# Third attention of a fused network: output stores on GpSimd's queue, relative products moved within a head, transposes of the probabilities three steps behind

## What is computed

```python
def _L2_attn_ref(x, Wq, Wk, Wv, Wo, pek, pev):   # HD = 8, MAX_LEN = 128, SCALE = HD ** 0.5
    Q, K, V = (proj(Wq), proj(Wk), proj(Wv))
    scores = jnp.einsum('bhqd,bhkd->bhqk', Q, K) / SCALE
    idx = _rel_idx(s)                            # clip(k - q, -128, 128) + 128
    rel_k = pek[idx]
    scores = scores + jnp.einsum('bhqd,qkd->bhqk', Q, rel_k) / SCALE
    scores = jnp.where(causal[None, None], scores, -jnp.inf)
    attn = jax.nn.softmax(scores, axis=-1)
    out = jnp.einsum('bhqk,bhkd->bhqd', attn, V)
    rel_v = pev[idx]
    out = out + jnp.einsum('bhqk,qkd->bhqd', attn, rel_v)
    return out.transpose(0, 2, 1, 3).reshape(b, s, D) @ Wo.T
```

## Time and profile before

| | us |
|---|---|
| Median of 3 runs | 4655.31 (4641.95 to 4663.07) |
| The profiled execution, its own time | 4653.93 |
| Its span | 4652.1 |
| The stage `relative_heads`, about | 2555 to 3527 of the span |

### The profile page before, as it was taken

One profiled execution on the slowest core, in us unless ns is written; L12 is line 12 of the kernel. 1 busy time (PEld: TensorE's weight loads), 2 busy tenths in 40 slices (PEclk: granted clock), 3 DMA queues, 4 the chain that ended last, 5 costly groups with the idle time before them and its releaser, 6 DMA issues. The chain is left out here.

```text
span 4652.1 us, 70787 instructions
## 1 busy us (share of the span) xinstructions
PE 3257.9 (70%) x22883; PEld 1799.3 (39%) x22883; DVE 2404.9 (52%) x4948; ACT 1877.1 (40%) x4450; POOL 684.5 (15%) x964
## 2 busy tenths in 40 slices
PE   5588544374435777778775777777783288849998
PEld 3344233253322444444443333333332122227776
DVE  4565466455655666666642445445455488821111
ACT  2355322211113455554542444444441177723332
POOL 2100000120003444444422000000000300000000
PEclk8798766686667899999986666666665599969999
DMA  4323000000001000000004777777772522220000
GB/s 118 64 48 62 23 0 0 8 1 5 0 9 47 17 17 9 17 17 17 17 9 138 188 190 192 190 192 191 193 195 72 137 42 53 40 69 1 0 0 18
DMA packets 423549, 303.19 MB, mean 65 GB/s; under 512 B 60175, under 2 KB 396234, under 8 KB 423250
## 3 DMA queue, kind: packets, MB, share of 16 engines
q1 hardware_dynamic: 414034, 278.32, 24.3%
q0 software_dynamic: 6912, 18.88, 1.3%
q10 hardware_dynamic: 2304, 2.36, 0.2%
HBM read 148.98 MB, written 133.18 MB: 61 GB/s over the span
## 5 line engine op out<-in xcount | busy, mean ns | idle before, releaser
L1139 DVE TENSOR_REDUCE a_soft_NM<-a_soft_s_ps 128x2 f32<-128x1024 f32 (+3 forms) x512 | 514.5, 1021 | 204.2 <-PE a_soft_s_ps L1074 132.3
L1173 ACT ACTIVATE a_soft_PTS<-a_soft_st_ps 128x512 f32<-128x512 f32 (+3 forms) x1024 | 458.3, 522 | 148.1 <-PE a_soft_st_ps L1050 100.9
L464 PE MATMUL a_soft_pt_ps<-net_ident,a_soft_PR 128*128 128x128 f32 x1280 | 328.7, 369 | 110.0 <-ACT a_soft_PTS L566 103.5
L612 ACT ACTIVATE a_soft_PR<-a_soft_s_ps,a_soft_least 128x128 f32<-128x128 f32 (+3 forms) x512 | 263.7, 526 | 342.3 <-DVE a_soft_least L587 237.9
L1045 PE MATMUL a_soft_st_ps<-a_soft_QS,a_soft_KS 50*128 50x512 bf16 (+4 forms) x1024 | 258.7, 360 | 59.4 <-ACT a_soft_PTS L1173 33.3
L1954 ACT ACTIVATE f_run_HT<-f_run_h_ps 128x512 f32<-128x512 f32 x256 | 152.8, 597 | 290.7 <-PE f_run_h_ps L1921 290.7
L1968 DVE SCALAR_TENSOR_TENSOR net_X<-f_run_y_ps,f_COEF,net_X 128x128 f32 x256 | 72.1, 344 | 381.2 <-PE f_run_y_ps L1930 381.2
L464 PEld LDWEIGHTS a_soft_pt_ps<-net_ident,a_soft_PR 128*128 128x128 f32 x1280 | 182.6, 180 | 208.7 <-ACT a_soft_PR L612 146.2
L1930 PEld LDWEIGHTS f_run_y_ps<-f_W,f_run_HT 128*128 128x128 f32 x2048 | 237.5, 192 | 26.8 <-issue 26.8
L1087 PE MATMUL a_soft_o_ps<-a_soft_PTS,a_soft_VR 128*32 128x512 f32 (+3 forms) x2048 | 242.6, 548 | 0.1
L2104 PE MATMUL f_run_ps<-f_run_WQKV,f_run_HT 128*128 128x512 f32 x384 | 229.6, 689 | 15.5 <-DVE f_run_RS L1402 8.3
(11 more groups left out here) (356 smaller groups left out, 6517.4 us busy)
## 6 DMA issues: line engine op xcount, KB each, us to landing
a_soft_BIAS<-skew_d SPq DMA_DIRECT2D x256, 191.0 KB, 4.2
band_d<-a_soft_PR SPq DMA_DIRECT2D x256, 191.0 KB, 3.7
skew_d<-a_soft_RS SPq DMA_DIRECT2D x128, 256.0 KB, 4.4
a_soft_PB<-band_d SPq DMA_DIRECT2D x128, 256.0 KB, 3.1
a_soft_QS<-query_rows_d SPq DMA_DIRECT2D x32, 384.0 KB, 9.6
query_rows_d<-a_proj_PARTS SPq DMA_DIRECT2D x72, 128.0 KB, 3.5
query_rows_d<-a_proj_PARTS POOLq DMA_DIRECT2D x72, 128.0 KB, 3.0
key_rows_d<-a_proj_PARTS SPq DMA_DIRECT2D x72, 128.0 KB, 3.9
```

The lines of the kernel that those rows point to most:

```text
L464: last = pe.transpose(pt_ps[:, slot, kb * P:(kb + 1) * P], PR[:, n % NPR, OFF + kb * P:OFF + (kb + 1) * P], ident[:])
L612: act.activation(PR[:, n % NPR, OFF:OFF + width(j)], s_ps[:, n % 4, 0:width(j)], ACT.Exp, bias=least[:, n:n + 1], scale=-1.0).then_inc(pro ...
L1139: dve.tensor_reduce(NM[:, T % 2, j, p, :], s_ps[:, ring["s", a] % 2, :, 0:width(j)], AX.X, ALU.max, negate=True).then_inc(max_ready, 1)
L1173: act.activation(PTS[:, T % 2, 2 * p + par, kb, q0:S], st_ps[:, e % 3, q0:S], ACT.Exp, scale=scale).then_inc(probs_ready, 1)
```

## The change

Four things move. The stores of the outputs are issued by GpSimd (POOL) instead of ACT, one quad at a time, after ACT has copied them. PE makes the relative products in step 3 of a head instead of step 0, and ACT copies them after the exponential of step 3 instead of before that of step 1. SP stores them after the stores of the band instead of before the load of a bias. And PE turns the probabilities three steps behind instead of two (`LAG`); which of a head's five turns falls to DVE and which to ACT stays as it was by position, so each engine gets other widths. No work is added or dropped.

```diff
@@ sync: quad
-                    for f, a in ((store_rel, 3), (load_bias, 2)):
-                        if not (final and h + a >= 4):
-                            f(hd + a, (h + a) % 4, qd if h + a < 4 else qd + 1)
+                    if not (final and h >= 2):
+                        load_bias(hd + 2, (h + 2) % 4, qd if h < 2 else qd + 1)
                     store_band(hd, h, qd)
+                    if not (final and h >= 1):
+                        store_rel(hd + 3, (h + 3) % 4, qd if h < 1 else qd + 1)
@@ gpsimd
-            batches(quad, lambda: None, pool)
+                if prev:
+                    store(qd - 1, 1 - u % 2, *((b, u - 1) if u else (b - 1, 3)))
+
+            def store(qd, sl, b, u):
+                pool.wait_ge(o_copied, qd + 1)
+                for h in range(4):
+                    pool.dma_start(out_d[ds(b, 1), 4 * u + h].rearrange("a r f -> (a r) f"),
+                                   OS[32 * h:32 * h + HD + 1, sl, :]).then_inc(o_stored[sl], 16)
@@ tensor: quad
-                    if j == 0 and not (final and h >= 1):
+                    if j == 3 and not (final and h >= 1):
                         uu, hh = (u, h + 3) if h < 1 else ((u + 1) % 4, h - 1)
                         relative(b if h < 1 or u < 3 else b + 1, uu, hh, 4 * qd + h + 3)
...
-                    if n >= 2:
-                        turn(qd, n - 2, h, pos, qd)
+                    if n >= LAG:
+                        turn(qd, n - LAG, h, pos, qd)
                     elif prev:
-                        turn(qd - 1, n + 14, h, pos, qd)
+                        turn(qd - 1, n + 16 - LAG, h, pos, qd)
@@ scalar: quad
-                        act.wait_ge(pt_ready, before(4 * qd + h - 2, 4 + j))
+                        act.wait_ge(pt_ready, before(4 * qd + h - 2, (5, 6, 7, 9)[j]))
...
-                    if j == 1 and not (isinstance(b, int) and qd == 4 * B - 1 and h >= 1):
-                        copy_rel(4 * qd + h + 3, (h + 3) % 4, qd if h else qd - 1)
                     act.activation(PR[:, n % NPR, OFF:OFF + width(j)], s_ps[:, n % 4, 0:width(j)], ACT.Exp,
                                    bias=least[:, n:n + 1], scale=-1.0).then_inc(probs_ready, 1)
                     copies(act, 1, qd, sl, n, prev)
+                    if j == 3 and not (isinstance(b, int) and qd == 4 * B - 1 and h >= 1):
+                        copy_rel(4 * qd + h + 3, (h + 3) % 4, qd if h else qd - 1)
                     if prev and n == 15:
-                        store(qd - 1, 1 - sl, b, u)
+                        copy_outputs(qd - 1, 1 - sl, b, u)
...
-                act.wait_ge(o_copied, qd + 1)
-                bb, uu = (b, u - 1) if u else (b - 1, 3)
-                for h in range(4):
-                    act.dma_start(out_d[ds(bb, 1), 4 * uu + h].rearrange("a r f -> (a r) f"),
-                                  OS[32 * h:32 * h + HD + 1, sl, :]).then_inc(o_stored[sl], 16)
```

More of the change, by code:

```diff
@@ L279, in relative_heads @@
     NPT = 5
+    LAG = 3
     NDMA = 2
@@ L285, in missing @@
     def missing(seq, slots):
-        return sum(m < seq and m % 2 in slots for m in (0, 1, 2, 7))
+        return sum(m < seq and m % 2 in slots for m in (0, 1, 2, 3, 7))
     def before(hd, pos):
@@ L291, in before @@
             return 5 * hd + pos - missing(5 * hd + pos, (0, 1))
-        return 5 * hd + pos - 4
+        return 5 * hd + pos - 5
     def through(qd, h, pos):
@@ L298, in through @@
             return seq // 2 - missing(seq, ((5 * h + pos) % 2,))
-        return 10 * qd + (5 * h + pos) // 2 - 2
+        return 10 * qd + (5 * h + pos) // 2 - 2 - (5 * h + pos) % 2
     with Scope(nc, stage) as s:
@@ L439, in quad, with last @@
                                  vall[:, ds(qd, 1), :, :].rearrange("p a h (j d) -> p (a h) j d", d=HD)).then_inc(vr_ready, 1)
-            batches(quad, lambda: None, pool)
+                if prev:
[5 more added lines that the diff above has]
+                                   OS[32 * h:32 * h + HD + 1, sl, :]).then_inc(o_stored[sl], 16)
+            def last():
+                store(4 * B - 1, 1, B - 1, 3)
+                for o in o_stored:
+                    pool.wait_ge(o, 64 * 2 * B)
+            batches(quad, last, pool)
         def q_blk(sl, h, j):
@@ L473, in turn_band, with pv @@
                 last.then_inc(pt_ready, 1)
-            def pv(qd, sl, kb, turned=2):
+            def pv(qd, sl, kb, turned=(2, 1)):
                 if kb == 0:
-                    pe.wait_ge(pt_copied[0], 10 * (qd + 1) + turned)
-                    pe.wait_ge(pt_copied[1], 10 * (qd + 1) + turned)
+                    pe.wait_ge(pt_copied[0], 10 * (qd + 1) + turned[0])
+                    pe.wait_ge(pt_copied[1], 10 * (qd + 1) + turned[1])
                     pe.wait_ge(vr_ready, qd + 1)
@@ L527, in last @@
             def last():
-                turn(4 * B - 1, 14, 0, 0, 4 * B)
-                turn(4 * B - 1, 15, 0, 1, 4 * B)
+                turn(4 * B - 1, 13, 0, 0, 4 * B)
+                turn(4 * B - 1, 14, 0, 1, 4 * B)
                 turn_band(4 * B - 1, 2, 0, 4 * B)
-                turn_band(4 * B - 1, 3, 0, 4 * B, 3)
+                turn(4 * B - 1, 15, 0, 3, 4 * B)
+                turn_band(4 * B - 1, 3, 0, 4 * B, 4)
                 for kb in range(NPT):
-                    pv(4 * B - 1, 1, kb, 0)
+                    pv(4 * B - 1, 1, kb, (1, -1))
             for hd in range(3):
@@ L548, in copies @@
                         copy_out(eng, slot, qd, h, pos, sl if h >= 2 else 1 - sl, (h + 2) % 4, None)
-                elif n >= 2:
-                    copy_out(eng, slot, qd, h, pos, sl, (n - 2) // 4, n - 2)
+                elif n >= LAG:
+                    copy_out(eng, slot, qd, h, pos, sl, (n - LAG) // 4, n - LAG)
                 elif prev:
-                    copy_out(eng, slot, qd, h, pos, 1 - sl, 3, n + 14)
+                    copy_out(eng, slot, qd, h, pos, 1 - sl, 3, n + 16 - LAG)
         def copy_out(eng, slot, now, h, pos, sl, head, n):
@@ L591, in last @@
             def last():
-                copy_out(dve, 0, 4 * B, 0, 0, 1, 3, 14)
+                copy_out(dve, 0, 4 * B, 0, 0, 1, 3, 13)
                 copy_out(dve, 0, 4 * B, 0, 2, 1, 2, None)
+                copy_out(dve, 0, 4 * B, 0, 4, 1, 3, None)
             batches(quad, last, dve)
@@ L614, in quad, with copy_outputs @@
                     copies(act, 1, qd, sl, n, prev)
+                    if j == 3 and not (isinstance(b, int) and qd == 4 * B - 1 and h >= 1):
+                        copy_rel(4 * qd + h + 3, (h + 3) % 4, qd if h else qd - 1)
                     if prev and n == 15:
-                        store(qd - 1, 1 - sl, b, u)
-            def store(qd, sl, b, u):
+                        copy_outputs(qd - 1, 1 - sl, b, u)
+            def copy_outputs(qd, sl, b, u):
                 if not (isinstance(qd, int) and qd < 2):
@@ L640, in last @@
             def last():
-                copy_out(act, 1, 4 * B, 0, 1, 1, 3, 15)
-                copy_out(act, 1, 4 * B, 0, 3, 1, 3, None)
-                store(4 * B - 1, 1, B, 0)
-                for o in o_stored:
-                    act.wait_ge(o, 64 * 2 * B)
+                copy_out(act, 1, 4 * B, 0, 1, 1, 3, 14)
+                copy_out(act, 1, 4 * B, 0, 3, 1, 3, 15)
+                copy_outputs(4 * B - 1, 1, B, 0)
             for hd in range(3):
```

## The result

The changed kernel took 4669.3 us (median of 15 runs, 4655.1 to 4675.7), the kernel before 4648.5 us in the runs beside it (median of 15, 4634.2 to 4663.1). The ratio is 1.0040 with a 95% interval of 1.0029 to 1.0051, that is some 19 us slower. The forecast was 54 us faster. The time lies inside the stated range of 4550 to 4680, in the case of "within 0.5%" that had 0.21.

The account below looks back on a forecast made before the run. SP's ring through the band stores' landing was taken as the bound. The quad falls from 29.9 to 28.1 us (27.7 on SP plus 0.4 of waits), 1.8 x 30 = 54 us off 4653.9, giving 4600; range 4550 to 4680.

Parts of the forecast that it names:

- within 0.5%: Whole kernel: time within about 0.5% (23 us) of the kernel before, no change measurable; chance 0.21.
- What bounds the kernel: SP's queue: a ring through the landing of its band stores, 28.9 us a quad, 29.5 with waits for ACT.
- The round of 7.0 us: SP's queue, kernel before: band load to next band load 7.01 us, of which 2.58 issuing and 4.4 band stores.
- SP's order: SP's queue: `skew_d` store moved behind band stores makes the round 6.7 us, the quad 27.7 on SP.
- the landing of the `skew_d` store: SP's new ring: store behind two band stores lands in 3.6 us, bounded by 3.1 and 4.6.
- Rival (a): SP's ring: `skew_d` store lands as before, 4.2 to 4.3 us; time 4650, no change; 0.21 together with (d).
- The end of the stage: Stage end: POOL's output stores are on the path once, costing under 1 us, below the sum's error.
- PE and ACT: Engines: PE's 2.4 us a quad of key waits go, ACT's stores leave, copy hidden, third step given nothing.
- rival (d): PE: SP isn't the bound, uneven turns eat the stall's gain; quad 29.9 us, 4654; 0.21 together with (a).
- What would show it: Profile signs: rounds near 6.7 us, new `skew_d` wait 0.3 to 1 us a head, POOL copies 28.1 us apart, DMA share 0.77.
- two signs against me: Profile: `skew_d` store landing above 4.2 us, or SP's waits for ACT growing to several us a quad.
- Rival (b): SP's bias load: new wait decides, landing 4.6 us, round 7.7, time 4708; loss when landing passes 4.3; chance 0.12.

## Why the prediction was wrong

**What bounds the kernel.** Right. SP's ring through the landing of the band's stores is the bound: taking that wait out of it gave 45 us, and taking 240 KB from beside the band 87 in the changed kernel. Also right: PE's wait for the keys goes, ACT's 2 us go, ACT's copy stays hidden from the `skew_d` store, and POOL can issue in its idle time. Two readings were too narrow. The round of 7.0 us, taken for what SP needs, is a short one: the median of the heads is 7.33. And SP's 18.0 us of waits for ACT aren't its only waits for engines; the same view has

```profile
SPq L376 <- DVE a_soft_least L587: 15.0, 31, 2.0
SPq L385 <- ACT a_soft_PR L612: 4.6, 7, 1.7
```

so that the three are 37.6 us, 1.3 a quad.

**SP's order: the failed step.** The round was forecast as 3.1 us and the landing of the `skew_d` store. The form of it held: 1.45 + 1.42 + 0.1 = 3.0, and 4.2 of landing, make 7.2, near the 7.5 a head that was measured. The term that was mis-sized is the landing: 3.6 forecast, 4.2 measured, 2.4 us a quad. The working of it began with the band's landing "in the last quad", 4.08 us, and laid the store's own 1.1 us behind that. This takes the queue for a line in which what comes later costs the earlier nothing, and it starts from a round that has no `skew_d` store at all. In the trace the median over all heads was 4.56 already before, and became 4.89 with the store behind the band, 0.8 more than the 4.08. The store then landed only some 0.7 us after the band (4.2, less the 3.5 from its issue to the next band load), not 1.1. So both landed late: the band load went out late and the bias load waited half a microsecond more. I had seen that loads issued behind the band delay it (4.3 against 3.6) and counted it for the start of a quad alone, as 0.9, when the change puts 256 KB there in every head. A second, smaller term fell short as well: SP's waits for engines, put at 0.4 us a quad, were 25.0 + 12.0 + 6.8 = 43.8 us, 1.5 a quad. They fill the gap from 7.2 to 7.5. Rival (a) had the landing at 4.25 and came out at 4650: that is the case that happened, for the quads.

The rule of the Trainium skill that was weighed there ("DMA: Bandwidth & Descriptors", section "Queues, rings and completion order": each DMA engine takes one ring's descriptors in order) would have let nothing behind the band hold it up. The pair of 4.18 and 4.89 us speaks against using it for landings. The Trainium skill itself adds, in the same section, that a later descriptor may finish its write before an earlier one.

**The end of the stage.** "Under 1 us" was wrong: 11.5 us in the profile, 7 to 8 in the ratios. The trace of before had the price of the landing from GpSimd's queue (3.0 us) but no row in which that queue is the last thing of a stage whose end others wait for in the same way, and I took the landing for the whole. By the ratios it is 7 to 8 of the 19 us. The rest, some 11 us, are the quads, as the run with only the last quad's stores from ScalarE shows by its ratio of 1.0024; the profiled execution of the changed kernel doesn't show them (29.90 a quad).

**PE and ACT.** The 2.4 us a quad of PE's stall did go, but became a wait for the band, since SP's ring stood still. To give the third step nothing by itself was near enough for the kernel as changed. With SP out of the way it costs 40 us, which I had only named as a possibility in rival (d).

**What would show it.** The new wait ahead of the bias load was there, 0.5 us each, as was the vanished wait for the keys. Rounds of 6.7 us, copies of POOL 28.1 apart and a DMA share of 0.77 didn't come (medians of 7.37 and copies 29.9 apart, share 0.72). Of the two signs against me, a `skew_d` landing above 4.2 us, the first was reached and not passed (4.2); SP's waits for ACT didn't grow (18.8 us, 0.6 a quad).

**Rival (b)**, slower because the landing passes 4.3 us, had the kind of outcome right and the turning point too high: alone, SyncE's order came out 23 us slower with the landing at 4.2. With 1.5 us a quad of waits instead of 0.4 the sum turns at 4.1. The time of 4669 lies in the stated range by the width of that range, which was drawn for a gain and a loss alike; the forecast of 4600 was 69 us off.

**Open.** Why the stage's end takes 13.2 us behind GpSimd's last stores. Their data moved between 3522 and 3524 in the profile, and from there to 3536 no compute engine works; the one entry is 0.10 us of POOL, the end of its issues (columns as in the earlier trace rows):

```profile
3523.00:3536.00 13.00, 0.00 (x0) 0.00 (x0) 0.00 (x0) 0.00 (x0) 0.10 (x1) 0.59 0.01 3
```

## What to carry to other kernels

When a transfer that nobody waits for soon is moved behind one that bounds a ring, don't take the landing of the first from a round in which the other is missing: with DMA engines busy three quarters of the time, "behind" isn't free. Here it was 0.8 us more than such a round had shown. Better to take the waiting instruction out of the issuer's way, by putting those issues ahead of it that hang on nothing late. And look at who is last before a stage ends, apart from what it costs in the loop.

## What the runs showed of the hardware

The landing of a transfer depends on what else its queue carries close by, ahead or behind. From the band stores (two of 191 KB) to the next band load it took 4.18 us (median) with a 16 KB store issued 1.4 us behind them and 4.89 with one of 256 KB; with that store in its old place, ahead of them, 3.90 and 4.56.

A stage whose last transfers were issued by GpSimd passed on 13.2 to 13.3 us after the last issue (four profiles), against 2.6 to 2.7 with ScalarE's (three). Where GpSimd's last issue ended 16.1 or 15.7 us ahead of the next stage's first load and ScalarE issued last, no such time was seen.

Four issues of 18 KB took GpSimd 1.97 to 2.25 us, and ScalarE 1.38 to 2.41 in the kernel before. PEclk was 0.67 to 0.69 between 2620 and 3400 in all fourteen kernels, with heads of 6.8 as with heads of 7.8 us.
